# The last additions of a mixture-of-experts kernel, given to GpSimd in place of VectorE

## The reference

```python
x = x + L0_conv(ln_channels(x)); t = to_tokens(x); t = t + L0_moe(ln_tokens(t)); x = from_tokens(t)
x = x + L1_conv(ln_channels(x)); t = to_tokens(x); t = t + L1_moe(ln_tokens(t)); x = from_tokens(t)

def moe(v):                                        # L1_moe; w and idx: the two chosen experts of a token
    h = gelu(einsum("nd,edf->enf", v, w1) + b1)
    y = einsum("enf,efd->end", h, w2) + b2
    return w[:, 0] * y[idx[:, 0]] + w[:, 1] * y[idx[:, 1]]
```

## Time and profile before

| | us |
|---|---|
| median of three runs | 990.66 |
| lowest and highest of the runs | 990.3 and 993.0 |
| the profiled execution | 989.66 |
| its span, first to last instruction | 986.8 |
| VectorE, ScalarE, GpSimd busy in the span | 555.5, 520.6, 608.4 |

### The profile page before, as it was taken

The page is one execution under the profiler, slowest core; times in us unless marked ns, Lnnn a source line. Parts: engine busy times, 40 slices in busy tenths (PEclk is TensorE's granted clock), DMA queues, the critical chain, the costliest instruction groups (busy, mean ns, idle before and its releaser), DMA issues.

```text
span 986.8 us, 14530 instructions
## 1 busy us (share of the span) xinstructions
PE 758.5 (77%) x4233; PEld 656.6 (67%) x4233; DVE 555.5 (56%) x1262; ACT 520.6 (53%) x1407; POOL 608.4 (62%) x597
## 2 busy tenths in 40 slices
PE   0766249999988798975789499976689977988760
PEld 0535238988887586864788387865679866776760
DVE  7967953263500198999867198999985004100005
ACT  1602427475565465653177376653287754555644
POOL 1000057777777777888632777888754777777760
PEclk9886569999999989999589699998699999999985
DMA  9000255455578483544136773543147856656537
GB/s 356 5 0 1 85 204 160 133 176 162 198 238 286 120 308 128 175 149 129 43 106 227 236 257 123 179 150 126 41 119 237 287 193 220 202 160 239 181 101 255
DMA packets 56861, 165.23 MB, mean 167 GB/s; under 512 B 13888, under 2 KB 13901, under 8 KB 56528
## 3 DMA queue, kind: packets, MB, share of 16 engines
q1 hardware_dynamic: 38608, 128.87, 38.5%
q0 software_dynamic: 18176, 35.44, 12.0%
HBM read 134.89 MB, written 31.20 MB: 168 GB/s over the span
## 4 chain that ended last, share of the span: by engine, by line
DVE 32%; PE 31%; POOL 16%; issue 8%; DMA 6%; ACT 5%; SPq 1%; POOLq 0%; DVEq 0%; ACTq 0%
PE h_ps L787 9%; POOL xg L515 8%; PE yT_ps L800 8%; POOL y_rows L524 8%; DVE state L1290 6%; DVE work L1276 5%; DVE work L1271 5%; DVE tok L1240 4%; PE acc_ps L739 4%; DMA xg<-xn_rows,tile_rows 3%; PE turn_ps L722 3%; PE acc_ps L759 3%; DVE work L1284 2%; DMA work<-y_rows 2%; DVE work L986 2%
## 5 line engine op out<-in xcount | busy, mean ns | idle before, releaser
L515 POOL DMA_INDIRECT xg<-xn_rows,tile_rows x284 | 301.5, 1062 | 226.7 <-DVEq L1206 123.8
L524 POOL DMA_INDIRECT y_rows<-yr,tile_rows x284 | 302.4, 1065 | 127.7 <-issue 82.3
L787 PE MATMUL h_ps<-xT,expert 128*128 128x256 f32 (+1 forms) x1376 | 295.3, 365 | 6.8 <-ACT hT L600 5.5
L600 ACT ACTIVATE hT<-h_ps,expert 128x256 f32<-128x256 f32 (+1 forms) x688 | 250.3, 442 | 72.0 <-PE h_ps L787 71.7
L800 PE MATMUL yT_ps<-hT,expert 128*128 128x256 f32 (+1 forms) x1376 | 278.8, 350 | 1.8 <-ACT yT L611 1.8
L787 PEld LDWEIGHTS h_ps<-xT,expert 128*128 128x128 f32 x1376 | 235.3, 205 | 29.3 <-issue 6.6
L800 PEld LDWEIGHTS yT_ps<-hT,expert 128*128 128x128 f32 x1376 | 233.7, 197 | 27.8 <-ACT yT L611 2.2
L1240 DVE SCALAR_TENSOR_TENSOR tok<-work,share,tok 128x128 f32<-128x128 f32 x224 | 62.3, 348 | 293.0 <-DMA work<-y_rows 292.3
L611 ACT ACTIVATE yT<-yT_ps,expert 128x256 f32<-128x256 f32 (+1 forms) x172 | 72.5, 440 | 116.7 <-PE yT_ps L800 116.6
L776 PE MATMUL xT_ps<-ident,xg 128*128 128x128 f32 x284 | 60.2, 294 | 88.4 <-DMA xg<-xn_rows,tile_rows 85.1
L588 ACT ACTIVATE xT<-xT_ps 128x256 f32<-128x256 f32 x144 | 55.6, 386 | 129.1 <-PE xT_ps L776 129.0
(11 more groups left out here) (202 smaller groups left out, 654.3 us busy)
## 6 DMA issues: line engine op xcount, KB each, us to landing
expert<-in_experts SPq DMA_DIRECT2D x172, 514.5 KB, 3.9
work<-y_rows SPq DMA_DIRECT2D x48, 256.0 KB, 6.2
xn_rows<-work SPq DMA_DIRECT2D x16, 512.0 KB, 6.3
xg<-xn_rows,tile_rows POOLq DMA_INDIRECT x284, 3.5
y_rows<-yr,tile_rows POOLq DMA_INDIRECT x284
tok<-in_x_tokens SPq DMA_DIRECT2D x8, 512.0 KB, 7.4
state<-in_x SPq DMA_DIRECT2D x2, 2048.0 KB, 17.4
work<-y_rows SPq DMA_DIRECT2D x8, 512.0 KB, 6.2
```

Source lines behind the costliest of these rows:

```text
L515: pool.indirect_dma_start(xg[:, s, h, :], None, xn_rows[unit], bass.IndirectOffsetOnAxis(ap=tile_rows[unit % 2][:, 0, at, h:h + 1], axis=0)) \
L524: pool.indirect_dma_start(y_rows[unit], bass.IndirectOffsetOnAxis(ap=tile_rows[unit % 2][:, 1, at, h:h + 1], axis=0), yr[:, s, h, :], None ...
L600: ins = act.activation(hT[:, s, c, cols], h_ps[c // 2][:, c % 2, cols], func, bias=expert[:, t.load(h) % W_RING, BIAS + c:BIAS + c + 1])
L787: mm = pe.matmul(h_ps[c // 2][:, c % 2, cols], expert[:, t.load(h) % W_RING, c * P:(c + 1) * P], xT[:, t.slot(2), cols], start=True, stop= ...
```

## The change

For the last unit VectorE no longer adds the second choice. It multiplies and adds the first choice only, and its fourth instruction of a piece raises a new semaphore, `s_first_in`. GpSimd, after its last scatter, waits for each piece on `s_first_in` and on ScalarE's `s_shared`, adds ScalarE's product to the tokens in one `tensor_tensor` of 128x512, and raises a second new semaphore, `s_last_in`. SyncE's stores of the last unit wait for that one. VectorE's waits on its own last product and on `s_shared` go away for this unit.

```diff
@@ store_image(b)
-                    sp.wait_ge(s_ln, combined(u) + (q + 1) * GROUPS // PIECES[u])
+                    if u == UNITS - 1:
+                        sp.wait_ge(s_last_in, q + 1)
+                    else:
+                        sp.wait_ge(s_ln, combined(u) + (q + 1) * GROUPS // PIECES[u])
@@ block.gpsimd, at its end
+            u = UNITS - 1
+            for q in range(PIECES[u]):
+                pool.wait_ge(s_first_in, q + 1)
+                pool.wait_ge(s_shared, q + 1)
+                ap = tok[u % IMAGES][:, piece(u, q), :]
+                pool.tensor_tensor(ap, ap, work_tok[CHOICES][:, piece(u, q), :], ALU.add).then_inc(s_last_in, 1)
@@ combine(u), on VectorE
                         if k == CHOICES - 1 and u == UNITS - 1:
-                            dve.wait_ge(s_shared, q + 1)
-                            ap = tok[b][:, piece(u, q), :]
-                            groups.step(dve.tensor_tensor(ap, ap, work_tok[1 + k][:, piece(u, q), :], ALU.add))
                             continue
...
-                        if k < CHOICES - 1:
+                        if u == UNITS - 1:
+                            ins.then_inc(s_first_in, 1)
+                        elif k < CHOICES - 1:
                             op(ins)
```

More of the change, by code:

```diff
@@ L374, in build @@
         s_shared = sem("last_outputs_times_shares")
+        s_first_in = sem("first_choice_of_last_outputs_added")
+        s_last_in = sem("second_choice_of_last_outputs_added")
         s_done = sem("output_stored")
```

## The result

The changed kernel takes 997.55 us in the median against 988.97 of the kernel before in the same series (22 runs of each). The ratio is 1.0058, with an interval of 1.0033 to 1.0082: **slower by 0.6%**, that is 3 to 8 us. (The ratio leaves out four of the 22 runs after, as disturbed, which the median keeps, so the two need not agree.) The profiled execution after took 994.71 us, its span is 992.9.

What follows compares the result with a forecast made beforehand. VectorE's own rate was taken to bound the tail; products 1.13 plus addition 1.20, fully excluding, put the last addition at 988.06 against 984.31, +3.75 us: 993.4 profiled, 994.4 forecast with 1.0 for the median, range 988.7 to 996.5.

Steps and rivals of the forecast that it cites:

- What bounded the end: Tail of the kernel before: from the third piece VectorE's own rate, 1.776 us a piece; no gain above about 2.5 us.
- Full exclusion: Last unit: VectorE's products and GpSimd's additions run one engine at a time; +3.75 us, 994.4 us, chance 0.60.
- Side by side: Rival for the last unit: no exclusion, GpSimd's additions follow ScalarE; -1.7 us, 988.9 us, chance 0.18.
- One-sided exclusion: Rival: GpSimd waits for one product an addition, VectorE never waits; 1.46 us a piece, -0.8; chance 0.15 with partial exclusion.
- its partial form: Rival: only a product's streaming part excludes GpSimd's addition; 1.73 us a piece, +0.15; chance 0.15 with the one-sided case.
- The row of the undisturbed product: VectorE's product took 336 to 423 ns beside indirect DMAs, 343 to 353 without; taken as speaking for no exclusion.
- The length of an addition: One GpSimd addition of 128x512 in the last unit: 1.20 us taken, bounds 0.58 and 1.27.
- the bound from the iota scaled to 512: Upper bound for a GpSimd addition: iota over 288 elements, 713 ns, scaled to 512 elements, 1.27 us.
- The cost of a piece: From the third piece on: VectorE's four products 1.13 us plus GpSimd's addition 1.20, together 2.33 us.
- with the store and the end behind it unchanged: Behind the last addition: the last store lands 2.0 us later, the span ends 2.5 us after, as before; no cost.
- nothing stands behind them there but its own additions and the end: GpSimd's two new waits in the last unit, behind its last indirect DMA: each priced at 0.10 us.
- the third rival: GpSimd late or longer: additions held till its drain ends at 971.8, +4.8 us, or lasting 1.5 us, +5.9; chance 0.07.

Runs made afterwards that it cites:

- the last experiment: The kernel before, with the first choice's product of the last piece moved from VectorE to ScalarE; ratio 0.9979 (0.9931 to 1.0027).

## Why the prediction was right or wrong

The sign was right, and of the two costs that the runs showed the prediction had the first and left out the second. As a ratio on the median of the runs shown then, 1.0058 is 996.4 us against the 994.4 forecast, just inside the range; the new median of 997.55 lies 1.05 above the range.

- *What bounded the end.* Right for the kernel before: VectorE's own rate, with ScalarE and the loads ahead. The late load in the last experiment shows how far one execution's tail can stray.
- *Full exclusion.* Right in the main: a product is held up for as long as an addition lasts (recorded from 973.16 to 974.51, the addition from 973.05 to 974.36). Side by side would have put the last addition 1.7 us earlier; it came 2.5 us later. One-sided exclusion had VectorE never wait, and it does. With bn_stats in place of the product the last addition did come at 17.95, 1.5 us earlier than before. But the 2.06 us a piece lie between the 2.33 of full exclusion and the 1.73 of its partial form (2.43 and 1.83 with an addition of 1.30), so how much of a product the addition shuts out is not settled by the pace. The row of the undisturbed product misled: what stood beside it there were indirect DMAs, which held a product up by far less (423 ns at most) than an addition does (1355). The Trainium skill (SBUF — State Buffer, section "Who interferes with whom") says that two-input VectorE instructions contend with a GpSimd instruction that reads SBUF and not with one that only writes it. The kernel after (1355 ns) and the one with memsets (353 ns at most) agree with it.
- *The length of an addition.* 1.20 was taken, 1.26 measured undisturbed and 1.30 in the kernel after. Near; the bound from the iota scaled to 512 (1.27) was the closest. The estimate from the Trainium skill (GPSIMD Engine Reference, section "Elementwise — side-by-side cycle accounting"), 1.12 us, was 0.14 too short.
- *The cost of a piece.* 2.33 was forecast (1.13 + 1.20), 2.06 measured: 0.27 too much, although the addition was longer. The step counted all four products outside of the addition. In the trace only 0.75 us lie between two additions: two of the next piece's four products are issued around the addition's start, and of these the second is recorded at about 1.35 us, which is the product kept waiting. The last addition so came at +2.5 us and not +3.75.
- *"with the store and the end behind it unchanged".* This is the step that failed, and it was the larger part. The store was unchanged (2.0 us to land); the end was not, as GpSimd's drain came 8.1 us behind its last addition. 5.8 us were forecast as nothing.
- *"nothing stands behind them there but its own additions and the end"* named the place and priced it at nothing. The row of the drain was even at hand, and the third rival used it the wrong way round: as something that an addition may have to wait for. The first addition began at 967.60, 0.15 us behind ScalarE's product and 6 us behind the last scatter: nothing held it. The length of the drain ought to have been read as a distance from GpSimd's last instruction, which moves with it: 8.1 us behind an addition that ends at 988 is an end at 996, and a forecast of 994.4 + 5.8 = 1000.2, or 999.0 with the 2.5 us that the additions cost.

So the total was near by two errors of unlike sign: 1.2 us too much for the exclusion, and nothing for the drain. In the profiled pair the whole is +8.4 us against +3.75 forecast. That 996.4 lies in the range is luck: no term of the sum stood for the drain, and the range reached up to 996.5 only for an addition of 1.5 us, which took 1.30.

## What to carry to other kernels

Before work is given to an engine that was idle at the end, look at what closes that engine: GpSimd with indirect DMAs behind it needed some 8 us of drain after its last instruction here, be it an addition, a memset or an indirect DMA, and this is free only while others are busy longer. Either let GpSimd end early, or put its drain where other work covers it. And VectorE and GpSimd, when both read two inputs, can cost more together than their lengths apart suggest, as here 2.06 us a piece where 1.32 was ScalarE's pace; the rows of both in one stretch tell it.

## What the runs showed of the hardware that was not expected

GpSimd's drain ended 8.1 us behind its last instruction in seven of the kernels (addition, memset or indirect DMA alike), 7.3 and 7.9 in the one with a drain halfway, and 0.07 us behind an addition when an explicit drain stood between the indirect DMAs and it. What GpSimd does in these 8 us no run shows.

A two-input product of VectorE that meets an addition on GpSimd is recorded as long (1.35 us for 0.34), with no wait shown: the idle time of VectorE in the tail doesn't grow, its mean duration does. Who looks only for gaps misses it.
